# A three-stage graph network kernel: the end of stages 1 and 2 rescheduled, and the first source indices of stages 2 and 3 loaded a stage ahead

## What is computed

```
def mean_agg(h): return segment_sum(h[src], dst, N) / max(degree, 1)
# network 1, two layers
h  = relu(x @ W_self1 + mean_agg(x) @ W_neigh1 + b1)          # 128 -> 150
h2 = h @ W_self2 + mean_agg(h) @ W_neigh2 + b2                # 150 -> 128
x1 = layernorm(x + h2)
# network 2, one message per edge
ef  = (relu(edge_attr @ We1 + be1) @ We2 + be2) * sigmoid(edge_weight @ Wt + bt)
msg = relu(concat(x1[src], ef) @ Wn1 + bn1) @ Wn2 + bn2
out = layernorm(x1 + segment_sum(msg, dst, N) + x1)
```

## Time and profile before

| | us |
|---|---|
| median of 3 runs | 7919.87 |
| the runs | 7901.61, 7919.87, 7921.28 |
| the profiled execution, its own time | 7915.53 |
| its span, first to last instruction | 7913.5 |
| mean granted clock of TensorE | 0.872 of full |

### The profile page before, as it was taken

How to read it: one execution, slowest core, us unless ns; L and a number is a source line. 1 busy time by engine, 2 the same in 40 slices (tenths; PEclk the granted TensorE clock), 3 DMA queues, 4 the chain that set the end, 5 groups by cost and what they waited for, 6 DMA issues and landing times.

```text
span 7913.5 us, 107196 instructions
## 1 busy us (share of the span) xinstructions
PE 5990.1 (76%) x32520; PEld 3929.6 (50%) x32520; DVE 5353.4 (68%) x11308; ACT 2436.9 (31%) x2998; POOL 5783.7 (73%) x5857
## 2 busy tenths in 40 slices
PE   5778888888767888887677777777777777777776
PEld 4555555555545555555444444444444444444444
DVE  8999988888645555554476666666666666666666
ACT  2111222222110000000244444444444444444544
POOL 7777776666647777776577777777777777777776
PEclk8889999999878988998788888888888888888888
DMA  4467777888768988999544444444444444444443
GB/s 124 145 206 230 250 255 264 283 277 283 260 210 295 305 304 303 312 311 305 176 126 131 128 133 129 133 130 130 129 136 130 134 133 132 134 135 133 135 134 100
DMA packets 651269, 1523.95 MB, mean 193 GB/s; under 512 B 162961, under 2 KB 346917, under 8 KB 643014
## 3 DMA queue, kind: packets, MB, share of 16 engines
q1 hardware_dynamic: 463491, 1133.19, 42.7%
q0 software_dynamic: 187200, 383.76, 17.0%
HBM read 1374.92 MB, written 141.47 MB: 192 GB/s over the span
## 4 chain that ended last, share of the span: by engine, by line
POOL 38%; issue 12%; DMA 0%; PE 0%; DVE 0%; ACT 0%; POOLq 0%; SPq 0%; DVEq 0%; ACTq 0%
POOL messages_rows L1708 38%; DMA messages_rows<-y_d,src_idx 0%; DVE messages_p_msg L1901 0%; PE messages_p_msg L1786 0%; PE messages_win L1747 0%; PE messages_p_hid L1780 0%; POOLq L1705 0%; ACT messages_gate L1822 0%; DMA messages_sums<-in_message_base 0%; PE messages_win L1548 0%; ACT messages_product L1831 0%; DVE messages_parts L1895 0%; PE messages_win L1765 0%; DVE messages_piece_stats L1563 0%; DVE messages_hot L1916 0%
## 5 line engine op out<-in xcount | busy, mean ns | idle before, releaser
L1708 POOL DMA_INDIRECT messages_rows<-y_d,src_idx x3125 | 3043.0, 974 | 1001.4 <-issue 948.5
L1112 POOL DMA_INDIRECT sum_x_rows<-in_x,sum_x_edges x1525 | 1577.2, 1034 | 621.0 <-issue 432.9
L1112 POOL DMA_INDIRECT sum_z_rows<-z_d,sum_z_edges x1200 | 1162.1, 968 | 477.4 <-issue 347.9
L1786 PE MATMUL messages_p_msg<-Wm_e,messages_gated 128*128 128x128 f32 x6250 | 1013.8, 329 | 498.9 <-DVE messages_below L1911 498.4
L1786 PEld LDWEIGHTS messages_p_msg<-Wm_e,messages_gated 128*128 128x128 f32 x6250 | 936.8, 237 | 878.1 <-issue 876.8
L1901 DVE TENSOR_TENSOR messages_p_msg<-messages_p_msg,messages_rows 128x1024 f32<-128x1024 f32 x391 | 481.4, 1231 | 1214.5 <-DMA messages_rows<-y_d,src_idx 1023.9
L1216 PE MATMUL sum_x_build<-sum_x_key_hot,sum_x_low_hot 128*128 128x490 bf16 (+2 forms) x2900 | 826.9, 371 | 304.6 <-DVE sum_x_counts L1412 290.9
L1818 ACT ACTIVATE messages_parts<-messages_p_msg 128x1024 bf16<-128x1024 f32 x391 | 400.1, 1023 | 1815.0 <-DVE messages_p_msg L1901 1815.0
L1236 PE MATMUL sum_z_p_loaded<-sum_z_split,sum_z_counts 128*128 128x384 bf16 x2744 | 797.0, 348 | 152.9 <-DMA sum_z_split<-z_parts_d 147.7
L1798 PE MATMUL messages_p_edge<-messages_hid,We 128*128 128x512 f32 x1564 | 812.2, 645 | 0.0
L1236 PE MATMUL sum_x_p_prod<-sum_x_split,sum_x_counts 128*128 128x385 bf16 x2744 | 690.9, 344 | 103.7 <-DMA sum_x_split<-x_parts_d 78.4
(11 more groups left out here) (273 smaller groups left out, 9064.1 us busy)
## 6 DMA issues: line engine op xcount, KB each, us to landing
sum_x_split<-x_parts_d SPq DMA_DIRECT2D x392, 675.5 KB
sum_z_split<-z_parts_d SPq DMA_DIRECT2D x392, 675.5 KB
messages_when<-in_edge_weight SPq DMA_DIRECT2D x391, 512.0 KB, 4.0
messages_attr<-in_span_attr SPq DMA_DIRECT2D x391, 256.0 KB, 4.3
counts_d<-sum_x_counts SPq DMA_DIRECT2D x392, 224.0 KB
sum_z_counts<-counts_d SPq DMA_DIRECT2D x56, 1568.0 KB
messages_rows<-y_d,src_idx POOLq DMA_INDIRECT x3125
sum_x_rows<-in_x,sum_x_edges POOLq DMA_INDIRECT x1525
```

What stands on the lines that cost most here:

```text
L1112: nc.gpsimd.indirect_dma_start(out=rows[:, s % depth, j, :], out_offset=None, in_=table, in_offset=bass.IndirectOffsetOnAxis(ap=edges[:, b ...
L1708: nc.gpsimd.indirect_dma_start(out=rows[:, g % SPAN_DEPTH, j, :], out_offset=None, in_=d["y"], in_offset=bass.IndirectOffsetOnAxis(ap=src_ ...
L1786: last = nc.tensor.matmul(p_msg[:, j * P:(j + 1) * P], gated[:, g % SPAN_GATEDS, j * P:(j + 1) * P], t.Wm_e[:], start=True, stop=True)
```

## The change

In `make_plan`, ring pieces are ready 2 slots after their group and not 4; the last flat piece, which no counted block touches (`plan.touched` is 13 in stage 1, 19 in stage 2), is ready like a ring piece; pieces that start late (from slot 260 in stage 1) are 4 slots apart; and the pass of stage 1's last block takes 6 slots and not 9. In stage 1 SP loads a piece's features in step 1 and not 0. Two small tables, `second_src` and `third_src`, are loaded by SP in slot 5 of stages 1 and 2; the first five groups of stage 2 and the first three of stage 3 are gathered by them, so POOL waits for no load there. A wait in stage 3 for a later load counts 64 and not 48. The guard on the last block becomes touched*256-128.

```
-SPAN_LOADS, SPAN_AHEAD = 4, 3
+SPAN_LOADS, SPAN_AHEAD, SPAN_FIRST = 4, 3, 3
+SPACING_LATE, LATE = 4, 30
...
-            plan.passes.append(([b], from_, min(26, plan.block_end[b + 1] - from_ - 2) if b + 1 < plan.blocks else 9))
+            plan.passes.append(([b], from_, min(26, plan.block_end[b + 1] - from_ - 2) if b + 1 < plan.blocks else 6))
...
+    def gathered_by(k):
+        tile = tiles * sqrt(min((PIECE * (k + 1) + 80) / m.N, 1.1))
+        return min(int((tile - end) / TILES) + 2, plan.groups)
...
-        if k < flat:
+        if k < flat and from_ < plan.blocks:
...
-            tile = tiles * sqrt(min((PIECE * (k + 1) + 80) / m.N, 1.1))
-            ready.append(min(int((tile - end) / TILES) + 4, plan.groups + 2))
+            ready.append(gathered_by(k))
+    plan.touched = len(plan.first_block)
+    if plan.touched < flat:
+        ready[flat - 1] = gathered_by(flat) + 1
...
-        slot += spacing
-    plan.slots = plan.start[plan.order[-1]] + PIECE_STEPS
+        slot += spacing if slot < units_by - LATE else SPACING_LATE
+    plan.slots = max(plan.start[plan.order[-1]] + PIECE_STEPS, plan.groups + 2)
...
     def sync(sp, n, k, s):
-        if s == 0:
+        if s == 1:
             load(sp, n, k)
...
-                if q == 0:
+                if q == 0 and (first or body):
                     pool.wait_ge(edges_in[body % EDGES_RING], 16 * (body // EDGES_RING + 1))
...
+                if s == UNROLL and first:
+                    sp.dma_start(t.second_src[:], d["edges"][:, second_from // BODY, 0]).then_inc(next_in, 16)
+                if s == UNROLL and not first:
+                    sp.dma_start(t.third_src[:], d["src_tiles"][:, 0:SPAN_FIRST * SPAN]).then_inc(next_in, 16)
...
-                if g in (0, SPAN_SOON):
-                    pool.wait_ge(keep_in[1 if g else 0], 48)
+                if g in (SPAN_FIRST, SPAN_SOON):
+                    pool.wait_ge(keep_in[0 if g == SPAN_FIRST else 1], 48 if g == SPAN_FIRST else 64)
```

26 lines of the change are left out of this document (16 added, 10 removed).

## The result

| | us |
|---|---|
| kernel before, median of 5 runs (lowest to highest) | 7920.75 (7901.61 to 7931.01) |
| changed kernel, median of 5 runs (lowest to highest) | 7881.96 (7878.78 to 7894.34) |
| ratio, with its 95% interval | 0.9957 (0.9945 to 0.9969) |
| profiled execution of the changed kernel: time, span | 7878.78, 7877.1 |

The change makes the kernel 0.43% faster, 34 us by the ratio and 36.4 us between the two spans (7913.5 and 7877.1). The forecast was 14.7 us, 7905, and its range ended at 7889. The sign was right, the size was not, and most of the gain sits in a place that the sum had at nothing. Ratios are of fast executions; a single one in all the experiments was slow (10962.33 us at a granted clock of 1.00, of the last kernel with step 6 moved) and stands in no ratio and no median here.

What follows compares the result with a forecast made beforehand. Stage 3 was taken as bound by POOL's gathers, stage 1 by DVE, transfers, then a chain, stage 2 by compute and transfers. Terms -10.2 + 5.4 + 1.5 - 0.4 - 6.9 + 2.5 - 6.6 = -14.7 gave 7905, range 7889 to 7922.

Steps and rivals of the forecast that it cites:

- piece 13 at slot 36: Early stage 1, where DVE is full: moving this piece there loses 5.4 us, bounds 4.2 and 11.0.
- later pieces sooner: Stage 1 ahead of slot 290: extra steps of pieces 43 and 44, partly hidden, lose 1.5 us, at most 5.6.
- turning to the end of stage 1: Behind the last product's turning: one piece less, three windows more, 49.3 us long, 10.2 saved, bounds 6.6 and 20.2.
- start of stage 2: Gathers start up to 4.2 us sooner, but only 0.4 us is gained, bounds 0 and 4.2.
- middle of stage 2: Piece 19 moved to slot 34 loses 2.5 us, from 1.5 a piece to about 5.4 with all DVE work exposed.
- end of stage 2: One piece less stands behind the last gather: 6.9 us gained.
- start of stage 3: First gather comes sooner and POOL doesn't stop afterwards: 6.6 us gained, bounds 6.0 and 6.9.
- Rival C: Stage 1's tail: chains after the windows run at 1.2 GHz, tail gives 6.6 us, sum -11.1, 7909; chance 0.09.
- D: Rival: stores queue behind the load of xT, ACT's copy waits; six pieces cost 30 us, sum +15, 7935; chance 0.06.
- rival A: End of stage 1: chunks load faster, the pass ends earlier, tail gives 20.2 us, sum -24.7, 7895; chance 0.20.
- Rival B: Stage 2's earlier gathers count if its compute is tied to rows: 3.8 us more, 7901; chance 0.07.
- E: Rival: data miss the guard on block 27, stage 1 is computed again, thousands of us more; chance 0.01.

Runs made afterwards that it cites:

- the last kernel with step 6 moved: Plan of changed kernel with next turn 3, 7 or 11 slots from a start; step 6 moved to slot 7, PE's step 3 to 4: 7892.18 us, 0.9965.
- the best phase: Changed kernel, stage 2 pieces from slot 34 to 200 waiting until the next turn is 3, 7 or 11 slots away: 7887.45 us, 0.9961.
- the worst: Changed kernel, stage 2 pieces from slot 34 to 200 waiting until the next turn is 2, 6 or 10 slots away: 7916.04 us, 1.0002.
- filled ends: Changed kernel with useless matmuls behind the last windows of stages 1 and 2, where pieces run alone: 7884.67 us, 0.9946.

## Why the prediction was wrong

The traces of all kernels make it possible to size stage 1's terms better than one pair can: eight have before's plan of stage 1, eleven the changed one without filling at its end.

| term | forecast | measured | from |
|---|---|---|---|
| piece 13 at slot 36 | +5.4 | +7.7 (to slot 60, so with pieces 14 and 15 two slots sooner) | means of 8 and 11 traces, 429.6 and 437.3 |
| slot 60 to slot 291 (later pieces sooner) | +1.5 | -0.3 | same traces, 2148.6 and 2156.0 |
| slot 291 to the turning | 0 | -1.7 | 50.6 and 48.9 |
| turning to the end of stage 1 | -10.2 | -2.9 | 60.2 and 57.3 |
| stage 1 in all | -3.3 | +2.8 (sd of one trace 6 to 8); by times 0 | 2266.6 and 2269.4 |
| start of stage 2 (first window behind ACT's first) | -0.4 | 0 | 15.9 before, 15.3 to 16.5 with the loads |
| middle of stage 2 | +2.5 | about -25 | means of three traces of each plan, 1140.2 and 1115.4 |
| end of stage 2 | -6.9 | -6.8 | 42.5 and 35.7, last gather to ACT's first |
| start of stage 3 | -6.6 | -5.8 | 6.9 and 1.1 |

**The step that failed** is the sentence on stage 2 that takes what the change does there to be one piece less at the end and one piece more at slot 34. The two slots by which every ring piece comes sooner were not costed at all: the prediction treats a piece's price as a property of the piece (1.5 to 5.4 us, wherever it stands), and a shift of all of them by the same amount as free. The runs show a price that depends on where its steps stand against the passes: 23 us for these two slots (0.9993 to 0.9964), and 29 us by the medians for one slot between the best phase and the worst. Nothing in the lines by group could have shown that, because they average over the phase. What could have is the count of ages at turns, which the two plans give (ten against one of age 6), and a table of slot lengths beside it, since nearly the whole difference lies in the three slots around each turn (18.3 and 16.9 us).

**"Bound its cost from both sides" was not done for it.** Piece 19's bounds (0 to 5.4) stood for the whole stage. A bound for the shift from rows was at hand: in the kernel before PE is idle for 5.8 of the 18.3 us that the three slots around a turn take on average (3.4 to 10.8 of them), and that 21 times. That would have moved the low end by 20 us or more, and with it the range, which missed the time by 7 us.

**End of stage 1: right in mechanism, too large.** Transfers pace the pass (47.8 us in 6 slots, under the 49.5 taken, above the 45 that would have disproved it), three more windows stand behind it, one piece less. But the rounds were sized by rounds that ran at full clock before, and nothing promised that clock after the change. Rival C had priced the half clock at 3.6 us more, and the trace has 3.6 us in the third round (11.17 for 7.6); 2.1 and 2.3 us came on top in the two rounds with windows. In the first of them PE waits 1.84 us for ACT's one-hot, and L1215 then runs at half clock too (2219.41, 2.37 us for 1.3); in the second the step 4 at its head does (L750 1.20 us for 0.67). 0.8 came ahead of the first piece. 57.9 is beyond the 53 at which the prediction names C or D; ACT waits for no store there, so it is C. The filled ends confirm that the clock's share is 7 us. That they come out at 50.2 us, near the 49.3 of the forecast, is luck: their rounds take 12.9, 12.4, 9.1 and 7.3 us and 5.6 to the end, where the sum had 10.8, 10.1, 7.6, 9.1 and 9.5.

**A result faster by over 0.3%** had a chance of 0.20, most of it through rival A, whose reason did not happen. **Rival B** was wrong in its condition too: gathers of stage 2 did not start sooner by more than the spread. In 19 kernels with the loads POOL's first one stands 3.3 to 4.6 us behind ACT's first instruction, 4.2 before. Taking away the wait that the profile names brought nothing that shows; what holds POOL until about then is in no row. At stage 3 the same edit gave 5.8 of 6.6, since there the wait for indices really was the last. Rivals D and E did not occur.

**POOL's waits in stage 2** were to grow by 4 us, and they fell from 58.1 to 26.8. The windows held the gathers up less, which fits a compute side that had become faster; the sum had looked for the change elsewhere.

**Right**: the end of stage 2 and the start of stage 3 (12.6 of 13.5 us), the price of piece 13 and its neighbours (7.7 us, within the bounds of 4.2 and 11.0), the pacing by transfers, and that loading xT a step later costs nothing that can be seen.
